# A GNN kernel's edge-count matrix: 32 source blocks of 100 instead of 40 of 80, laps of 8 groups, and two VectorE instructions a lap

## The chip, the cores and the metric

The kernel runs on one core of one Trainium2 chip. The metric is the device time of one execution in microseconds (us). "Before" was timed three times: 2426.53, 2431.27 and 2434.8 us, a median of 2431.27 us.

## The reference

There are 3125 nodes with 128 features and 103,125 edges, sorted by destination. Four graph layers run one after the other, each added to its input and layer-normalised:

```python
x = _layernorm(x + relu(segment_sum(edge_weight[:, None] * (x @ W0)[src], dst) + b0))        # GCN
x = _layernorm(x + gat(x))        # 4 heads, softmax over the edges into each dst, skip, layernorm
x = _layernorm(x + attention(x))  # Q,K,V, softmax over the edges into each dst; x + attn @ Wo
x = _layernorm(x + sage(x))       # two mean aggregations, relu between them, sigmoid at the end
```

All sums over edges are rewritten as products with dense 3200 x 3200 matrices (3125 padded to 3200, in 25 tiles of 128 rows). One holds how many edges lead from a source to a destination, one the sum of their weights.

## The kernel before

**Edge tables** (`edge_tables`, 0 to 81 us): the edge list is loaded, and for each group of WD = 3 destination rows the first 128 edges of the group are gathered. There are LAPS x LW = 1056 groups. A source number s is split into a high part hi = s // SL and a low part s % SL, with HI = 40 blocks of SL = 80. `k.near` holds five fields for each edge: the key (row in the group times HI plus hi, of KEYS = 120), the low part, and the edge weight as three bf16 pieces (PARTS = 3). The field is its outer dimension.

**Matrix build** (`build_matrices`, 81 to 450 us) runs LAPS = 88 laps of LW = 12 groups:

- DVE (`onehots`): one comparison makes the low one-hots (L483), one the key one-hots (L485), and three products (L489) multiply the low one-hots by the three weight pieces. Everything is double-buffered (RING = 2). The comparison waits on `used`, so for the PE of two laps before; the products wait on `lows`, which the first comparison sets.
- PE (`products`): for each group a matmul with the 128 key columns as weights and 160 moving columns (counts and first weight piece), and two more of 80 columns that add the other pieces. So 36 matmuls a lap, of which the last comes behind the check below.
- DVE and PE both call `beyond` in each lap: it reads two numbers of the table `k.before` into registers (L451) and compares them (L456). Only if some group has more than 128 edges does it do extra work, which doesn't occur in this execution. In the lap loop (`each_lap`, L446) two laps are unrolled.
- ACT (`copy_out`, L557) copies 120 partitions x 1920 results from PSUM to one of two `stage` buffers, after that buffer's last store has landed.
- SP (`store`, L566) stores the buffer in runs of 2 x 80 f32 (count and weight side by side, 640 bytes).

**Readers**: `aggregate` (449 to 610 us) multiplies the weight matrix with the features, 16 PE instructions for each of 25 tiles, from a ring of UN = 5 tiles. `gat_rows` and `attend_rows` load the counts, also in 25 tiles each. All three load through `load_rows` (L715), which gathers 80 f32 (320 bytes) at a time. The later `load_tiles` (L725) reads another matrix, which the change doesn't touch.

Of the kernel before, what the change touches and what calls it, by code (L numbers as in the profile page):

```python
# [14 lines left out]
BF16 = mybir.dt.bfloat16  # L15
I32 = mybir.dt.int32
I16 = mybir.dt.int16
ALU = mybir.AluOpType
# [3 lines left out]
P = 128  # L22
# [4 lines left out]
NP = NT * P  # L27
# [16 lines left out]
LASTN = E - FULL * P  # L44

WD = 3
HI = 40
SL = NP // HI
KEYS = WD * HI
LW = 12  # L50
LAPS = NP // (WD * LW)
ROWS = LAPS * LW * WD
WT = -(-(LAPS * LW + 1) // P)
NWP = WT * P
BATCHES = 3
PARTS = 3
RING = 2
# [49 lines left out]
def edge_tables(nc, k):  # L107

    with ExitStack() as ctx:
# [30 lines left out]
        start = sb("start", [P, WT])  # L140
# [3 lines left out]
        ids = sb("ids", [P, NWP], I32)  # L144
        weight = sb("weight", [P, NWP])
# [23 lines left out]
        WHOLE = (ECT - 1) * P  # L169
        TAIL = FULL - WHOLE  # L170
        N_PADS = 4
        N_CONSTS = 17
        BT = WT // BATCHES
        BW = BT * P

# [32 lines left out]
        def _(pool):  # L208
# [8 lines left out]
            pool.memset(k.ident[:, :], 0.0).then_inc(consts, 1)  # L217
            pool.memset(ahead[:, :], 0.0).then_inc(consts, 1)
            pool.memset(wrap[:, :], 0.0).then_inc(consts, 1)
            pool.memset(k.KEY[:, :, :, KEYS:P, :], 0.0).then_inc(consts, 1)  # L220
            pool.memset(k.zeros[:, :], 0.0).then_inc(consts, 1)
            pool.wait_ge(consts, 9)
            pool.affine_select(out=k.ident[:, :], in_=k.ident[:, :], compare_op=ALU.not_equal, fill=1.0,
                               base=0, pattern=[[-1, P]], channel_multiplier=1).then_inc(consts, 1)
            pool.affine_select(out=ahead[:, :], in_=ahead[:, :], compare_op=ALU.not_equal, fill=1.0,
# [4 lines left out]
                               base=P - 1, pattern=[[-1, P]], channel_multiplier=P).then_inc(consts, 1)  # L230
            pool.iota(base_i[:, :], pattern=[[KEYS, NWP]], base=0, channel_multiplier=0).then_inc(consts, 1)
            pool.iota(edge_i[:, :], pattern=[[P, ECOL]], base=0, channel_multiplier=1).then_inc(consts, 1)
            pool.iota(k.low_grid[:], pattern=[[1, SL], [0, 2]], base=0, channel_multiplier=0).then_inc(consts, 1)
            pool.iota(k.key_grid[:], pattern=[[1, KEYS], [0, 2]], base=0, channel_multiplier=0).then_inc(consts, 1)
            pool.wait_ge(rows_ready, 1)
            for t in range(WT):
                pool.indirect_dma_start(chunk_dst[:, t], None, k.dst.rearrange("(e a) -> e a", a=1),
# [7 lines left out]
                                        bass.IndirectOffsetOnAxis(ap=held_i[:, t:t + 1], axis=0)  # L245
                                        ).then_inc(k.own_in[t // BT], 16)
            pool.iota(k.iota_low[:, :], pattern=[[1, SL]], base=0, channel_multiplier=0)
            pool.iota(k.iota_key[:, :], pattern=[[1, P]], base=0, channel_multiplier=0)
            pool.memset(nought[:, :], 0.0).then_inc(noughts, 1)

        @block.vector
        def _(dve):
# [80 lines left out]
            for b in range(BATCHES):  # L333
                cols = slice(b * BW, (b + 1) * BW)
                dve.wait_ge(taken, 2 * (b + 1))
                unpack(ids[:, cols], weight[:, cols], BW, k.near[:, 0, cols], k.near[:, 1, cols],
                       [k.near[:, 2 + v, cols] for v in range(PARTS)], k.key_base[:, cols])

        @block.tensor
        def _(pe):  # L340
# [78 lines left out]
def build_matrices(nc, k):  # L419

    with ExitStack() as ctx:
        def sb(name, shape, dt=F32):
            return ctx.enter_context(nc.sbuf_tensor(name, shape, dt))

        def sem(name):
            return ctx.enter_context(nc.semaphore(name))

        OH = sb("bm_oh", [P, RING, LW // 2, 1 + PARTS, SL, 2], BF16)
        gate = sb("bm_gate", [P, 1])  # L430
        more_key = sb("bm_more_key", [P, P], BF16)
        more_oh = sb("bm_more_oh", [P, 1 + PARTS, SL], BF16)
        stage = sb("bm_stage", [KEYS, 2, LW, 2, SL])
        ps = ctx.enter_context(nc.psum_tensor("bm_ps", [P, 8, BANK], F32))
        used, lows, made, copied, more_step, more_made, more_used = map(
            sem, ("bm_used", "bm_lows", "bm_made", "bm_copied", "bm_more_step", "bm_more_made", "bm_more_used"))
        stored = [sem(f"bm_stored{s}") for s in range(2)]
        block = ctx.enter_context(nc.Block())
        WHY = "the tables' ranges lie inside the columns"
# [31 lines left out]
        @block.vector  # L471
        def _(dve):
            dve.sem_inc(more_used, 1)

            def onehots(lap, u, two):
                wide_low, wide_key = [P, LW // 2, SL, 2], [P, LW // 2, KEYS, 2]

                def spread(f, wide):
                    return (k.near[:, f, bass.ds(lap * LW, LW)].rearrange("p (a b) -> p a b", b=2).unsqueeze(2)
                            .to_broadcast(wide))  # L480

                dve.wait_ge(used, lap + 1)
                dve.tensor_tensor(OH[:, u, :, 0], k.low_grid[:].unsqueeze(1).to_broadcast(wide_low),  # L483
                                  spread(1, wide_low), ALU.is_equal).then_inc(lows, 1)
                dve.tensor_tensor(k.KEY[:, u, :, 0:KEYS], k.key_grid[:].unsqueeze(1).to_broadcast(wide_key),  # L485
                                  spread(0, wide_key), ALU.is_equal)
                dve.wait_ge(lows, lap + 1)
                for v in range(PARTS):
                    last = dve.tensor_tensor(OH[:, u, :, 1 + v], OH[:, u, :, 0], spread(2 + v, wide_low), ALU.mult)  # L489
                last.then_inc(made, 1)  # L490

                def more(at, w, c, b, i):
                    dve.wait_ge(more_used, at + 1)
                    dve.tensor_tensor(gate[:], k.edge_at[:, bass.ds(c, 1)], k.lim[:, bass.ds(w, 1)], ALU.is_ge
                                      ).then_inc(more_step, 1)
                    dve.tensor_scalar(more_key[:], k.iota_key[:], k.key_base[:, bass.ds(w, 1)],
                                      k.col_key[:, bass.ds(c, 1)], ALU.add, ALU.is_equal).then_inc(more_step, 1)
                    dve.tensor_scalar(more_oh[:, 0], k.iota_low[:], k.col_low[:, bass.ds(c, 1)], None, ALU.is_equal
                                      ).then_inc(more_step, 1)
                    dve.wait_ge(more_step, at * 3 + 3)  # L500
                    dve.tensor_scalar(more_key[:], more_key[:], gate[:], None, ALU.mult)
                    for v in range(PARTS):
                        last = dve.tensor_scalar(more_oh[:, 1 + v], more_oh[:, 0], k.col_parts[:, v, bass.ds(c, 1)], None,
                                                 ALU.mult)
                    last.then_inc(more_made, 1)

                beyond(dve, lap, more)

            each_lap(dve, onehots)

        @block.tensor
        def _(pe):
            pe.sem_inc(used, RING)
            pe.sem_inc(copied, 2)

            def products(lap, u, two):
                def place(i, v):
                    b, c = divmod(i, PER_BANK)
                    return ps[:, 4 * u + b, c * WIDE + SL * (v > 0):(c + 1) * WIDE]

                def body(i, planes):
                    a, b = divmod(i, 2)
                    for v in planes:
                        moving = OH[:, u, a, 0:2, :, b] if v == 0 else OH[:, u, a, 1 + v, :, b]
                        last = pe.matmul(place(i, v), k.KEY[:, u, a, :, b], moving, start=i % PER_BANK == 0 and v == 0,  # L525
                                         stop=True, skip_group_check=True)
                    return last

                pe.wait_ge(copied, lap + 1)
                pe.wait_ge(made, lap + 1)  # L530
                for i in range(LW - 1):
                    body(i, range(PARTS))
                body(LW - 1, range(PARTS - 1))

                def more(at, w, c, b, i):
                    pe.wait_ge(more_made, at + 1)
                    for v in range(PARTS):
                        out = ps[:, bass.ds(b + 4 * u, 1), bass.ds(i * WIDE + SL * (v > 0), WIDE - SL * (v > 0))]
                        out = out.rearrange("p b c -> p (b c)")
                        last = pe.matmul(out, more_key[:], more_oh[:, 0:2] if v == 0 else more_oh[:, 1 + v],  # L540
                                         start=False, stop=True, skip_group_check=True)
                    last.then_inc(more_used, 1)

                beyond(pe, lap, more)
                body(LW - 1, range(PARTS - 1, PARTS)).then_inc(used, 1)

            each_lap(pe, products)
# [1344 lines left out]
def program(nc, ins, out):  # L1892
# [16 lines left out]
    with ExitStack() as ctx:  # L1909
        def sb(name, shape, dt=F32):  # L1910
            return ctx.enter_context(nc.sbuf_tensor(name, shape, dt))
# [4 lines left out]
        with ExitStack() as edges:  # L1916
            def esb(name, shape, dt=F32):
                return edges.enter_context(nc.sbuf_tensor(name, shape, dt))

            k.chunk_in = [ctx.enter_context(nc.semaphore(f"chunk_in{b}")) for b in range(BATCHES)]  # L1920
            k.own_in = [ctx.enter_context(nc.semaphore(f"own_in{b}")) for b in range(BATCHES)]
            k.near = esb("near", [P, 2 + PARTS, NWP], BF16)
            k.before = esb("before_row", [1, NWP], I32)
            k.first = esb("first_row", [1, NWP], I32)
            k.lim = esb("limits", [P, NWP])
# [3 lines left out]
            k.col_parts = esb("col_parts", [P, PARTS, ECOL])  # L1929
            k.key_base = esb("key_base", [P, NWP])  # L1930
            k.iota_low = esb("iota_low", [P, SL], I16)
            k.iota_key = esb("iota_key", [P, P], I16)
            k.low_grid = esb("low_grid", [P, SL, 2], I16)
            k.key_grid = esb("key_grid", [P, KEYS, 2], I16)
            k.KEY = esb("key_onehots", [P, RING, LW // 2, P, 2], BF16)
            edge_tables(nc, k)
            build_matrices(nc, k)
        deg = sb("deg", [P, NT])
# [50 lines left out]
```

## Time and profile before

| | |
|---|---|
| timed runs | 2426.53, 2431.27, 2434.8 us |
| profiled execution's own time | 2439.62 us |
| its span (first to last instruction) | 2437.9 us |
| mean granted TensorE clock | 0.900 of full speed |
| busy share PE, PEld, DVE, ACT, POOL | 78%, 59%, 72%, 46%, 5% |
| first L483 to last build matmul | 81.3 to 440.9 us |
| first to last `aggregate` matmul start | 459.2 to 609.5 us |

The profile is one execution, so every duration in it comes from that one. Busy time is summed over the span; an idle stretch of an engine is put down to the engine or DMA whose semaphore event came last, which for a wait behind register work can name the wrong one. Matmuls overlap, so their durations don't add up to busy time.

### The profile page before, as it was taken

The numbers are of one execution on the slowest core, as the hardware profiler recorded it, in microseconds if no ns is written. First come the engines' busy times: TensorE is split into PE (matmuls) and PEld (weight loads), VectorE is DVE, ScalarE is ACT, GpSimd is POOL, SyncE is SP. The second block draws the span as 40 slices with busy tenths as digits, with TensorE's granted clock in tenths as the row PEclk, the third lists the DMA queues.
The fourth block names the chain that finished last, engine by engine and source line by source line (L and its number), as shares of the span: only waits on it lengthen the run. The fifth ranks groups of instructions, "written<-read, shape, count | busy, mean of one in ns | idle before, by whom it ended". The sixth has DMA issues, their size and how long they took to land. (4 is left out here: it accounts for less than half of the span.)

```text
span 2437.9 us, 44362 instructions
## 1 busy us (share of the span) xinstructions
PE 1902.0 (78%) x16121; PEld 1441.9 (59%) x16122; DVE 1753.2 (72%) x1874; ACT 1133.4 (46%) x1959; POOL 127.3 (5%) x225
## 2 busy tenths in 40 slices
PE   3456666699478888898888888873899999498794
PEld 2456555444456666676666667652688887354452
DVE  4887877100359999999999999855788885572375
ACT  1344444100257777677777777632666664101001
POOL 4000000000000000000000000000000000010120
PEclk6787877799689999999999999986899999699897
DMA  3488888999023443322444432211865650492492
GB/s 103 116 235 230 231 221 220 237 270 244 6 62 103 111 110 109 97 50 73 110 109 110 109 79 59 82 39 35 162 129 108 133 108 3 188 409 112 204 420 76
DMA packets 582353, 341.98 MB, mean 140 GB/s; under 512 B 397008, under 2 KB 574312, under 8 KB 575640
## 3 DMA queue, kind: packets, MB, share of 16 engines
q1 hardware_dynamic: 579928, 338.61, 50.4%
q0 software_dynamic: 720, 1.77, 0.3%
q10 hardware_dynamic: 1648, 0.83, 0.1%
q8 instruction: 37, 0.61, 0.1%
q14 instruction: 20, 0.16, 0.0%
HBM read 214.18 MB, written 127.01 MB: 140 GB/s over the span
## 5 line engine op out<-in xcount | busy, mean ns | idle before, releaser
L1207 ACT ACTIVATE exponentials<-gr_ps,att_cols 128x256 f32<-128x256 f32 (+1 forms) x1300 | 493.3, 491 | 185.1 <-PE gr_ps L1097 183.3
L1097 PE MATMUL gr_ps<-ident,gr_r 128*128 128x128 f32 x2500 | 381.8, 292 | 69.0 <-DVE gr_r L1315 67.0
L1097 PEld LDWEIGHTS gr_ps<-ident,gr_r 128*128 128x128 f32 x2500 | 284.1, 147 | 153.0 <-issue 130.8
L1128 PE MATMUL gr_ps<-exponentials,heads 128*33 128x128 f32 x5000 | 363.5, 277 | 14.1 <-DVE exponentials L1322 14.1
L1322 DVE SCALAR_TENSOR_TENSOR exponentials<-exponentials,gr_count_t 128x3072 f32<-128x3072 f32 (+1 forms) x104 | 349.0, 3355 | 21.9 <-ACT exponentials L1207 17.9
L1288 DVE CUSTOM_DVE_ANT_0 gr_unread<-gr_src_rows,gr_closed 128x3125 bf16<-128x3125 f32 (+1 forms) x100 | 344.2, 3442 | 17.0 <-ACT gr_closed L1200 16.6
L525 PE MATMUL bm_ps<-bm_oh,key_onehots 128*128 128x80 bf16 (+1 forms) x3168 | 228.9, 238 | 146.6 <-issue 119.4
L525 PEld LDWEIGHTS bm_ps<-bm_oh,key_onehots 128*128 128x128 bf16 x3168 | 202.7, 112 | 172.8 <-issue 169.3
L1128 PEld LDWEIGHTS gr_ps<-exponentials,heads 128*33 128x33 f32 x5000 | 254.1, 110 | 80.5 <-issue 55.9
L557 ACT ACTIVATE bm_stage<-bm_ps 120x1920 f32<-120x1920 f32 x88 | 156.0, 1773 | 220.8 <-DMA adjacency<-bm_stage 119.5
L798 PE MATMUL sage_ps<-sage_counts,sage_parts 128*128 128x400 bf16 x1200 | 207.4, 337 | 14.6 <-DVE sage_counts L832 14.6
L1315 DVE TENSOR_SCALAR gr_r<-gr_src_rows,gr_lift_u,gr_floor_u 128x3125 f32<-128x3125 f32 (+1 forms) x100 | 188.0, 1921 | 13.1 <-PE gr_ps L1097 7.5
L798 PEld LDWEIGHTS sage_ps<-sage_counts,sage_parts 128*128 128x128 bf16 x1200 | 118.6, 99 | 104.1 <-DVE sage_counts L832 16.0
L1546 PE MATMUL ar_ps<-KT,ar_left 128*128 128x400 f32 x400 | 147.1, 512 | 16.2 <-DVE ar_low_u L1637 14.7
L489 DVE TENSOR_TENSOR bm_oh<-bm_oh,near 128x960 bf16<-128x960 bf16 x264 | 157.4, 652 | 0.0
L698 PE MATMUL agg_gcn_ps<-agg_gcn_ring,agg_gcn_left 128*128 128x400 f32 x400 | 142.5, 512 | 14.3 <-DMA agg_gcn_ring<-adjacency 14.2
L1565 PEld LDWEIGHTS ar_ps<-ar_pt,X 128*128 128x128 f32 x1250 | 145.5, 192 | 11.5 <-ACT ar_pt L1609 4.5
L1565 PE MATMUL ar_ps<-ar_pt,X 128*128 128x128 f32 x1250 | 147.8, 275 | 0.0
L832 DVE CAST sage_counts<-sage_ring 128x3200 bf16<-128x3200 f32 x50 | 93.7, 1874 | 47.6 <-POOL sage_ring L788 47.6
L710 DVE COPY agg<-agg_gcn_ps 128x1600 f32<-128x1600 f32 x1 | 1.8, 1825 | 173.4 <-PE agg_gcn_ps L698 173.4
L698 PEld LDWEIGHTS agg_gcn_ps<-agg_gcn_ring,agg_gcn_left 128*128 128x128 f32 x400 | 75.6, 193 | 81.3 <-issue 30.6
L1609 ACT ACTIVATE ar_pt<-ar_ps 128x512 f32<-128x512 f32 (+1 forms) x175 | 84.0, 547 | 77.4 <-PE ar_ps L1555 77.4
(319 smaller groups left out, 1970.2 us busy)
## 6 DMA issues: line engine op xcount, KB each, us to landing
sage_ring<-count_by_source SPq DMA_DIRECT2D x50, 1600.0 KB, 9.3
adjacency<-bm_stage SPq DMA_DIRECT2D x88, 900.0 KB, 5.8
agg_gcn_ring<-adjacency SPq DMA_DIRECT2D x25, 1600.0 KB, 14.4
gr_count<-adjacency SPq DMA_DIRECT2D x25, 1600.0 KB, 9.3
ar_counts<-adjacency SPq DMA_DIRECT2D x25, 1600.0 KB, 9.1
count_by_source<-gr_count_t SPq DMA_DIRECT2D x12, 3200.0 KB, 16.7
fg_node<-gat_node_sums SPq DMA_DIRECT2D x1, 1650.0 KB, 6.3
count_by_source<-gr_count_t SPq DMA_DIRECT2D x1, 1600.0 KB, 7.1
```

What stands on the lines that cost most here:

```text
L489: last = dve.tensor_tensor(OH[:, u, :, 1 + v], OH[:, u, :, 0], spread(2 + v, wide_low), ALU.mult)
L525: last = pe.matmul(place(i, v), k.KEY[:, u, a, :, b], moving, start=i % PER_BANK == 0 and v == 0, stop=True, skip_group_check=True)
L557: act.activation(stage[:, u].rearrange("p (b w) v c -> p b (w v c)", b=BANKS), ps[0:KEYS, BANKS * u:BANKS * (u + 1), 0:PER_BANK * WIDE], A ...
L698: last = pe.matmul(ps[:, b, 0:CW], left[:, u, :], ring[:, u, b * CW:(b + 1) * CW], start=False, stop=True, skip_group_check=True)
L798: last = pe.matmul(ps[:, b, 0:CW], parts[:, u, i, :], counts[:, u, b * CW:(b + 1) * CW], start=False, stop=True, skip_group_check=True)
L1097: last = pe.transpose(ps[:, i % RINGS, c:c + P], r[:, j, s * P:(s + 1) * P], k.ident[:])
L1128: last = pe.matmul(ps[j * PAIR:j * PAIR + C + 1, 7, 0:P], heads[:, h, s, :], e[:, s, j * P:(j + 1) * P], start=s == 0, stop=s == NT - 1, s ...
L1207: last = act.activation(e[:, s, 0:w], ps[:, i % RINGS, c:c + w], ACT.Exp, bias=cols[:, h, s:s + 1])
L1288: dve.tensor_tensor_reduce(out=unread[:, 0:n], in0=src_rows[:, h, 0:n], in1=closed[:, j, 0:n], scale=1.0, scalar=FLOOR, op0=ALU.subtract, ...
L1315: last = dve.tensor_scalar(r[:, j, 0:n], src_rows[:, h, 0:n], lift_u[:, h, j:j + 1], floor_u[:, h, j:j + 1], ALU.add, ALU.max)
L1322: dve.scalar_tensor_tensor(part, part, 1.0, count_t[:, first:last, 0:w], ALU.min, ALU.mult).then_inc(weighed, 1)
L1565: last = pe.matmul(ps[:, 7, 0:P], k.X[:, first + j, :], pt[:, i, j * P:(j + 1) * P], start=first + j == 0, stop=first + j == NT - 1, skip_ ...
```

## The change

- HI goes from 40 to 32 and so SL from 80 to 100 and KEYS from 120 to 96. The stored run is 2 x 100 f32 (800 bytes), the run read by `load_rows` 100 f32 (400 bytes).
- LW goes from 12 to 8, LAPS from 88 to 132. The number of groups stays 1056 and `ROWS` 3168.
- The key one-hots get the same width (100) as the low ones and lie in the same tile, `hot`, and both come from one comparison against one grid. The three products become one instruction. That one waits for the comparison in front of it.
- The matmul's weights are 100 columns instead of 128, its moving columns 200, 100 and 100 instead of 160, 80 and 80; results lie in 100 PSUM partitions, of which 96 are copied.
- `k.near` gets the layout [group of 8 edges' columns, field, column], so that one access pattern spans several fields; the edge tables write it in pieces of 8.
- Two iotas and a memset go from the POOL queue.

```diff
-HI = 40
+HI = 32
-LW = 12
-LAPS = NP // (WD * LW)
+LW = 8
+LAPS = 2 * (NP // (2 * WD * LW))
...
-            pool.memset(k.KEY[:, :, :, KEYS:P, :], 0.0).then_inc(consts, 1)
...
-            pool.iota(k.low_grid[:], pattern=[[1, SL], [0, 2]], base=0, channel_multiplier=0).then_inc(consts, 1)
-            pool.iota(k.key_grid[:], pattern=[[1, KEYS], [0, 2]], base=0, channel_multiplier=0).then_inc(consts, 1)
+            pool.iota(k.grid[:], pattern=[[1, SL], [0, 2]], base=0, channel_multiplier=0).then_inc(consts, 1)
...
-            pool.iota(k.iota_key[:, :], pattern=[[1, P]], base=0, channel_multiplier=0)
...
-                unpack(ids[:, cols], weight[:, cols], BW, k.near[:, 0, cols], k.near[:, 1, cols],
-                       [k.near[:, 2 + v, cols] for v in range(PARTS)], k.key_base[:, cols])
+                mine = [k.near[:, b * (BW // LW):(b + 1) * (BW // LW), f, :] for f in range(2 + PARTS)]
+                unpack(ids[:, cols], weight[:, cols], BW, mine[0], mine[1], mine[2:], k.key_base[:, cols])
...
-        OH = sb("bm_oh", [P, RING, LW // 2, 1 + PARTS, SL, 2], BF16)
+        hot = sb("bm_hot", [P, RING, 2 + PARTS, LW // 2, SL, 2], BF16)
...
+                def over(fields):
+                    return [P, (fields.stop - fields.start) * (LW // 2), SL, 2]
+
+                def spread(fields):
+                    mine = k.near[:, bass.ds(lap, 1), fields].rearrange("p l f (a b) -> p (l f a) b", b=2)
+                    return mine.unsqueeze(2).to_broadcast(over(fields))
+
+                def planes(fields):
+                    return hot[:, u, fields].rearrange("p f a c b -> p (f a) c b")
+
+                both, parts = slice(0, 2), slice(2, 2 + PARTS)
                 dve.wait_ge(used, lap + 1)
-                dve.tensor_tensor(OH[:, u, :, 0], k.low_grid[:].unsqueeze(1).to_broadcast(wide_low),
-                                  spread(1, wide_low), ALU.is_equal).then_inc(lows, 1)
-                dve.tensor_tensor(k.KEY[:, u, :, 0:KEYS], k.key_grid[:].unsqueeze(1).to_broadcast(wide_key),
-                                  spread(0, wide_key), ALU.is_equal)
-                dve.wait_ge(lows, lap + 1)
-                for v in range(PARTS):
-                    last = dve.tensor_tensor(OH[:, u, :, 1 + v], OH[:, u, :, 0], spread(2 + v, wide_low), ALU.mult)
-                last.then_inc(made, 1)
+                dve.tensor_tensor(planes(both), k.grid[:].unsqueeze(1).to_broadcast(over(both)), spread(both), ALU.is_equal
+                                  ).then_inc(compared, 1)
+                dve.wait_ge(compared, lap + 1)
+                low = hot[:, u, 1].rearrange("p a c b -> p (a c b)").unsqueeze(1)
+                dve.tensor_tensor(planes(parts), low.to_broadcast([P, PARTS, LW * SL]), spread(parts), ALU.mult
+                                  ).then_inc(made, 1)
...
+                        moving = hot[:, u, 1:3, a, :, b] if v == 0 else hot[:, u, 2 + v, a, :, b]
+                        last = pe.matmul(ps[0:SL, BANKS * u + bank, c * WIDE + SL * (v > 0):(c + 1) * WIDE],
+                                         hot[:, u, 0, a, :, b], moving, start=c == 0 and v == 0, stop=True,
+                                         skip_group_check=True)
...
-            k.near = esb("near", [P, 2 + PARTS, NWP], BF16)
+            k.near = esb("near", [P, NWP // LW, 2 + PARTS, LW], BF16)
```

## Rows read from the trace of the kernel before

**Rows 1.** Groups of instructions, 81 to 450 us; line, operation, count, busy, mean ns, idle before.

```profile
L525 PE MATMUL bm_ps<-bm_oh,key_onehots 128*128 128x80 bf16 (+1 forms) x3168 | 228.9, 238 | 146.6 <-issue 119.4 <-DVE bm_oh L489 26.5
L489 DVE TENSOR_TENSOR bm_oh<-bm_oh,near 128x960 bf16<-128x960 bf16 x264 | 157.4, 652 | 0.0
L557 ACT ACTIVATE bm_stage<-bm_ps 120x1920 f32<-120x1920 f32 x88 | 156.0, 1773 | 220.8 <-DMA adjacency<-bm_stage 119.5 <-PE bm_ps L525 101.3
L485 DVE TENSOR_TENSOR key_onehots<-key_grid,near 128x1440 bf16<-128x1440 int16 x88 | 79.3, 902 | 0.0
L483 DVE TENSOR_TENSOR bm_oh<-low_grid,near 128x960 bf16<-128x960 int16 x88 | 57.9, 658 | 76.6 <-PE bm_ps L525 74.0 <-issue 1.4 <-PEq L513 1.0
```

**Rows 2.** Windows: build stage; stretch, length, busy by engine, PE clock, DMA share, GB/s.

```profile
81.20:441.20 360.00, 228.88 (x3168) 202.73 (x3168) 279.76 (x440) 154.26 (x88) 0.00 (x0) 0.80 0.81 220
```

**Rows 3.** Timeline, 199 to 217 us; start, duration, instruction, idle before.

```profile
199.53 0.66 DVE L483 TENSOR_TENSOR bm_oh<-low_grid,near 128x960 bf16<-128x960 int16 x1 [1.33 <-PE bm_ps L525]
202.64 0.65 DVE L483 TENSOR_TENSOR bm_oh<-low_grid,near 128x960 bf16<-128x960 int16 x1
202.86 1.88 PE L525 MATMUL bm_ps<-bm_oh,key_onehots 128*128 128x160 bf16 x35 [0.50 <-DVE bm_oh L489]
207.33 0.66 DVE L483 TENSOR_TENSOR bm_oh<-low_grid,near 128x960 bf16<-128x960 int16 x1 [1.52 <-PE bm_ps L525]
...
208.73 1.79 DVE L489 TENSOR_TENSOR bm_oh<-bm_oh,near 128x960 bf16<-128x960 bf16 x3
...
211.04 0.66 DVE L483 TENSOR_TENSOR bm_oh<-low_grid,near 128x960 bf16<-128x960 int16 x1 [0.52 <-PE bm_ps L525]
...
214.80 0.66 DVE L483 TENSOR_TENSOR bm_oh<-low_grid,near 128x960 bf16<-128x960 int16 x1 [0.58 <-PE bm_ps L525]
```

**Rows 4.** DVE's queue in the lap 207.2 to 210.9 us; ns min/median/max, first and last start.

```profile
L451 DVEq TENSOR_LOAD <-before_row x2: 431/706/980, 208.5 to 209.9; - x2
L456 DVEq COMPARE_BRANCH  x1: 56/56/56, 210.6 to 210.6; - x1
L483 DVEq FUSED_REGOPS  x1: 75/75/75, 210.9 to 210.9; - x1
```

**Rows 5.** DVE's queue in the next lap, 210.9 to 214.6 us.

```profile
L489 DVEq FUSED_REGOPS  x3: 57/57/57, 211.7 to 212.0; - x3
L451 DVEq TENSOR_LOAD <-before_row x2: 303/462/620, 212.3 to 213.4; - x2
L446 DVEq COMPARE_BRANCH  x1: 66/66/66, 214.3 to 214.3; - x1
```

**Rows 6.** Line 451 over the whole span, the queues of DVE and PE.

```profile
L451 DVEq TENSOR_LOAD <-before_row x176: 302/556/1370, 82.5 to 435.8; - x176
L451 PEldq TENSOR_LOAD <-before_row x176: 298/624/1487, 86.2 to 440.0; - x176
```

**Rows 7.** Line 451, 81 to 91 us, before and at the first store.

```profile
L451 DVEq TENSOR_LOAD <-before_row x6: 304/312/556, 82.5 to 90.5; - x6
```

**Rows 8.** The first comparison and the staging tile, whole span.

```profile
L483 DVE TENSOR_TENSOR bm_oh<-low_grid,near x88: 650/659/660, 81.3 to 433.5; 128x960 bf16<-128x960 int16 x88
L566 SPq DMA_DIRECT2D adjacency<-bm_stage x88: 329/330/377, 90.5 to 443.1; - x88
...
  DMA adjacency<-bm_stage: 119.5, 54
...
DMA to landing us min/median/max: 5.4/5.8/7.0
```

**Rows 9.** Groups of instructions, whole span: an ACT copy of 1536, two weight loads.

```profile
L1220 ACT ACTIVATE gr_count_t<-gr_ps 128x1536 f32<-128x1536 f32 x50 | 70.1, 1449 | 40.9 <-PE gr_ps L1106 40.9
L525 PEld LDWEIGHTS bm_ps<-bm_oh,key_onehots 128*128 128x128 bf16 x3168 | 202.7, 112 | 172.8 <-issue 169.3
L698 PEld LDWEIGHTS agg_gcn_ps<-agg_gcn_ring,agg_gcn_left 128*128 128x128 f32 x400 | 75.6, 193 | 81.3 <-issue 30.6
```

**Rows 10.** Windows of `aggregate`: three tiles from a full ring, fifteen in steady state.

```profile
467.30:483.40 16.10, 16.10 (x49) 9.04 (x48) 0.00 (x0) 0.00 (x0) 0.88 (x3) 1.00 1.25 272
508.40:598.55 90.15, 84.53 (x240) 44.42 (x240) 0.00 (x0) 0.00 (x0) 3.62 (x13) 1.00 1.24 272
```

**Rows 11.** ACT waits for the first count tiles of `attend_rows`, timeline.

```profile
1706.19 2.96 ACT L1598 ACTIVATE ar_closed<-ar_counts,ar_big 128x3200 bf16<-128x3200 f32 x1 [15.27 <-DMA ar_counts<-adjacency]
```

**Rows 12.** DVE waits for DMA in the edge tables, groups of instructions, 0 to 200 us.

```profile
L288 DVE CAST dst_f<-dst_i 128x903 f32<-128x903 int32 x1 | 0.6, 630 | 3.2 <-DMA dst_i<-in_dst_dram 3.2
L283 DVE TENSOR_TENSOR near<-scratch,near 128x384 bf16<-128x384 f32 x3 | 1.7, 559 | 0.1
```

More of the change, by code:

```diff
@@ L171, in edge_tables @@
         N_PADS = 4
-        N_CONSTS = 17
+        N_CONSTS = 15
         BT = WT // BATCHES
@@ L219, in _ @@
             pool.memset(wrap[:, :], 0.0).then_inc(consts, 1)
-            pool.memset(k.KEY[:, :, :, KEYS:P, :], 0.0).then_inc(consts, 1)
             pool.memset(k.zeros[:, :], 0.0).then_inc(consts, 1)
-            pool.wait_ge(consts, 9)
+            pool.wait_ge(consts, 8)
             pool.affine_select(out=k.ident[:, :], in_=k.ident[:, :], compare_op=ALU.not_equal, fill=1.0,
@@ L427, in sem @@
             return ctx.enter_context(nc.semaphore(name))
-        OH = sb("bm_oh", [P, RING, LW // 2, 1 + PARTS, SL, 2], BF16)
+        hot = sb("bm_hot", [P, RING, 2 + PARTS, LW // 2, SL, 2], BF16)
         gate = sb("bm_gate", [P, 1])
-        more_key = sb("bm_more_key", [P, P], BF16)
+        more_key = sb("bm_more_key", [P, SL], BF16)
         more_oh = sb("bm_more_oh", [P, 1 + PARTS, SL], BF16)
@@ L434, in build_matrices @@
         ps = ctx.enter_context(nc.psum_tensor("bm_ps", [P, 8, BANK], F32))
-        used, lows, made, copied, more_step, more_made, more_used = map(
-            sem, ("bm_used", "bm_lows", "bm_made", "bm_copied", "bm_more_step", "bm_more_made", "bm_more_used"))
+        used, compared, made, copied, more_step, more_made, more_used = map(
+            sem, ("bm_used", "bm_compared", "bm_made", "bm_copied", "bm_more_step", "bm_more_made", "bm_more_used"))
         stored = [sem(f"bm_stored{s}") for s in range(2)]
@@ L475, in onehots @@
             def onehots(lap, u, two):
[L476 to L480, printed above, removed]
-                dve.wait_ge(used, lap + 1)
-                dve.tensor_tensor(OH[:, u, :, 0], k.low_grid[:].unsqueeze(1).to_broadcast(wide_low),
-                                  spread(1, wide_low), ALU.is_equal).then_inc(lows, 1)
-                dve.tensor_tensor(k.KEY[:, u, :, 0:KEYS], k.key_grid[:].unsqueeze(1).to_broadcast(wide_key),
-                                  spread(0, wide_key), ALU.is_equal)
-                dve.wait_ge(lows, lap + 1)
-                for v in range(PARTS):
-                    last = dve.tensor_tensor(OH[:, u, :, 1 + v], OH[:, u, :, 0], spread(2 + v, wide_low), ALU.mult)
-                last.then_inc(made, 1)
+                def over(fields):
[6 more added lines that the diff above has]
+                both, parts = slice(0, 2), slice(2, 2 + PARTS)
+                dve.wait_ge(used, lap + 1)
+                dve.tensor_tensor(planes(both), k.grid[:].unsqueeze(1).to_broadcast(over(both)), spread(both), ALU.is_equal
[4 more added lines that the diff above has]
+                                  ).then_inc(made, 1)
                 def more(at, w, c, b, i):
@@ L495, in more @@
                                       ).then_inc(more_step, 1)
-                    dve.tensor_scalar(more_key[:], k.iota_key[:], k.key_base[:, bass.ds(w, 1)],
+                    dve.tensor_scalar(more_key[:], k.iota_low[:], k.key_base[:, bass.ds(w, 1)],
                                       k.col_key[:, bass.ds(c, 1)], ALU.add, ALU.is_equal).then_inc(more_step, 1)
@@ L516, in products @@
             def products(lap, u, two):
-                def place(i, v):
-                    b, c = divmod(i, PER_BANK)
-                    return ps[:, 4 * u + b, c * WIDE + SL * (v > 0):(c + 1) * WIDE]
                 def body(i, planes):
                     a, b = divmod(i, 2)
+                    bank, c = divmod(i, PER_BANK)
                     for v in planes:
-                        moving = OH[:, u, a, 0:2, :, b] if v == 0 else OH[:, u, a, 1 + v, :, b]
-                        last = pe.matmul(place(i, v), k.KEY[:, u, a, :, b], moving, start=i % PER_BANK == 0 and v == 0,
-                                         stop=True, skip_group_check=True)
+                        moving = hot[:, u, 1:3, a, :, b] if v == 0 else hot[:, u, 2 + v, a, :, b]
+                        last = pe.matmul(ps[0:SL, BANKS * u + bank, c * WIDE + SL * (v > 0):(c + 1) * WIDE],
+                                         hot[:, u, 0, a, :, b], moving, start=c == 0 and v == 0, stop=True,
+                                         skip_group_check=True)
                     return last
@@ L537, in more @@
                     for v in range(PARTS):
[L538 to L541, printed above, removed]
+                        out = ps[0:SL, bass.ds(b + BANKS * u, 1), bass.ds(i * WIDE + SL * (v > 0), WIDE - SL * (v > 0))]
+                        last = pe.matmul(out.rearrange("p b c -> p (b c)"), more_key[:],
+                                         more_oh[:, 0:2] if v == 0 else more_oh[:, 1 + v], start=False, stop=True,
+                                         skip_group_check=True)
                     last.then_inc(more_used, 1)
@@ L1931, in program @@
             k.iota_low = esb("iota_low", [P, SL], I16)
[L1932 to L1935, printed above, removed]
+            k.grid = esb("grid", [P, SL, 2], I16)
             edge_tables(nc, k)
```

## The prediction

> **What bounds the kernel now.** The change touches the build of the matrix, and through the layout the stages that read it, so I read the groups of the build first. 88 laps run from the first L483 at 81.3 to the last at 433.5 us [rows 8]: 352.2 / 87 = 4.05 us a lap, 356 us in all, 15% of the span. Neither the groups nor the window name an engine that is full: DVE is busy for 280 of 360 us, PE 229, ACT 154, the DMA engines 81% [rows 1, 2]. ACT waits 119.5 us for stores and 101.3 us for PE; DVE waits 74 us "for PE" [rows 1].
>
> The last is misleading. Follow one lap [rows 3, 4]. The comparisons start at 207.33 and the three products are through at 208.73 + 1.79 = 210.52, yet the next comparison starts at 211.04. PE isn't what holds it: DVE's own queue read a table entry from 209.9 for 0.43 us, branched at 210.6 and came to the next L483 at 210.9. The queue takes its items in turn: it dispatches the five instructions, the products only once the first comparison is complete, then makes `beyond`'s two reads and the branch, and only then enters the next lap. That lap took 3.71 us, of which the reads were 0.431 + 0.980 = 1.41 and the rest 2.30. The next lap, with the loop's branch, took 3.76 us: reads 0.92, rest 2.84 [rows 3, 5]. So a lap costs DVE's queue (2.30 + 2.84) / 2 = 2.57 us plus two reads. A read took 0.30 us before the first store [rows 7] and 0.556 us at the median of the stage, up to 1.37 [rows 6]. Were there no other wait, 4.05 - 2.57 = 1.48 us would be two reads; twice the median is 1.11. DVE's queue is thus busy for 3.7 to 4.05 of 4.05 us. PE's queue has the same reads (median 0.624, rows 6) and its own 36 matmuls; it isn't far behind. A staging buffer's round is copy 1.77, issue about 0.2, landing 5.8 us: 7.8 for two laps, 3.9 a lap [rows 1, 8]. Three loops of nearly one length, then, of which the first has a cost per lap, whatever a lap holds.
>
> **The change part by part.** I work against the profiled execution, 2439.6 us.
>
> *DVE in a lap.* By L483 and L485 an element costs (902 - 658) / 480 = 0.508 ns [rows 1]. The one comparison of 2 x 8 x 100 = 1600 elements takes 658 + 640 x 0.508 = 983 ns, the one product of 2400 takes 652 + 1440 x 0.508 = 1384 ns. That is 2.37 us of engine time a lap where the five took 0.66 + 0.90 + 3 x 0.65 = 3.52: fewer instructions, but the elements per group rise from 440 to 500. In the queue the product waits for a comparison of 0.98 instead of 0.66 us (+0.325), and two dispatches go; three of them start from 211.7 to 212.0, so 0.13 each [rows 5] (-0.26). The rest of a lap goes from 2.57 to 2.635 us. The two reads and the branch stay, because they are per lap. The product (1.38 us) lies beside them and costs nothing; it would cost only if the reads and the branch, 1.1 us plus at least 0.6, were gone.
>
> *The reads.* The floor is 2 x 0.30 = 0.61 us [rows 7], the ceiling the 1.48 of above. They are longer while stores run, and a store now has 48 packets an engine instead of 90 or more in a lap that is little shorter, so I take the middle, 1.05. Lap: 2.635 + 1.05 = 3.69 us; 132 laps 486 us, against 356: **+130 us**. Ends: 132 x 3.24 = 428 (+72) and 132 x 4.11 = 543 (+187).
>
> *PE in a lap.* 35 matmuls ran in 1.88 us for 12 groups of 320 columns [rows 3]; 8 groups of 400 columns are 3200 instead of 3840, so about 1.6 us warm and twice that at the lower clock level. Its period was within 4.05 with 12 matmuls more. It fits beside 3.69, and it gets slack, since the matmuls of a lap can start after 2.4 us of DVE's lap and not after 3.3. Zero; bounds 0 to +0.23 us a lap, inside the ends above. Should weights of 100 columns load more slowly, see below.
>
> *ACT and the store.* A copy of 1536 took 1449 ns, of 1920 1773 [rows 1, 9]: 0.84 ns an element, so 1600 take 1.50 us. The DMA share of 0.81 over 360 us and 16 engines for 88 x 120 x 12 = 126,720 runs [rows 2] is 36.8 ns a run of 640 bytes; 90 runs an engine are 3.3 us, and 5.8 - 3.3 = 2.5 us of the landing are fixed. A run of 800 bytes costs between 36.8 (by the run) and 46 ns (by the byte); 48 of them 1.8 to 2.2 us. Landing 4.5 us, round 1.5 + 0.2 + 4.5 = 6.2, so 3.1 us a lap: hidden under 3.69. Without that cover the stage would take 132 x 3.1 = 409 us.
>
> *Tail of the stage.* The last copy is 0.3 us shorter, the last landing 1.3: -1.6, say -2.
>
> *Readers.* Three tiles from a full ring took 16.1 us, 5.37 each; in steady state 15 tiles took 90.15, 6.01 each [rows 10], with PE idle in between at full clock: there the loads set the pace. A tile is 5120 runs of 320 bytes and becomes 4096 of 400. By the run that is 4.8 us, so PE's 5.37 would bound; by the byte nothing changes. About 20 tiles are paced so: 0 to -13 us; I take -10, nearer to the run, as the engines move 272 GB/s here in runs half the size of the store's. In `gat_rows` and `attend_rows` only the first loads are exposed, the clearest by 15.3 us [rows 11]; a tenth of it is -2 (0 to -4) in both together.
>
> *Edge tables.* The iotas and the memset that go leave DVE waiting for `dst_i` 3.2 us longer than for POOL [rows 12], so 0. The writes of `near` in pieces of 8 are made from f32 input at 559 ns for 384 elements, 1.45 ns each: slow already, so 0; were each of the 15 twice as long, +8.
>
> Sum: +130 - 2 - 10 - 2 = +116 us, 2555.6 us for a twin of the profiled execution. That one lay 8.3 us above the median, so I forecast 2431.3 + 116 = **2547 us**.
>
> **The rivals.**
>
> *A, the cost goes by the group (chance 0.07), and the change wins.* If DVE's and PE's queue work is hidden and what paces a lap is what it stores and computes, a lap of 8 groups takes 8/12 of 4.05 = 2.70 us and the stage stays at 356. The readers' and the tail's 14 us are left: 2417 us. For it: ACT waited for stores in 54 of 88 laps [rows 8]. Against it: laps of 3.71 and 3.76 us that the queue explains to the end. It decides from a lap below (356 + 14) / 132 = 2.80 us; the queue's fixed part alone is 2.6, and with two of the quickest reads 3.24.
>
> *B, quiet reads (0.15).* If the loops lock so that the reads fall between the stores, the lap is 3.24: +72 - 14, 2489 us. The lap from 199.53 to 202.64 took 3.11 us in the midst of the stage [rows 3], so quick laps exist. Against it: the median read of the stage is nearly twice the quiet one.
>
> *C, the staging round bounds (0.05).* If the reads take less than I think and the round of 3.1 us is the longest loop: 409 - 356 - 14 = +39, 2470 us.
>
> *D, weight loads (0.05).* A bf16 load of 128 columns averages 112 ns, an f32 load of the same 193 [rows 9]. If 100 columns lose the quick form, and a load's extra 50 to 90 ns can't hide behind matmuls of 100 columns, 24 of them add 1.2 to 2.2 us to PE's lap of at most 4.05 - 12 x 0.054 = 3.4, and a lap of about 5 us gives 660 - 356 - 14 = +290, 2721 us. The Trainium skill, "TensorE: Matmul & The Clock Gate", section "Weight-path perf modes", states just that condition: the quick weight load is on only for 128 weights that aren't f32. What no row says is whether the slow one shows; loads already lie beside matmuls (35 in a stretch of 1.88 us is 54 ns each, half of a load's own 112), hence the small chance.
>
> **How the numbers follow.** Main case 0.68. The range 2475 to 2625 takes in B and all but the last part of the main case's ends (2489 to 2604, and 20 us above for waits of DVE on the stores) and leaves out A, C and D, 0.17, and a little of the tails. A difference of 0.3% (7 us) is what a measurement can tell from none. Faster by more: 0.07 (A). Within: 0.02 (between A and C). Slower: 0.91.
>
> **What would show it.** In the profile after: 132 L451 pairs, still two reads a lap, of 0.3 to 1 us; from one comparison to the next 3.5 to 3.9 us with a DVE that is busy for only 2.3 of them and idle "for PE"; the two DVE instructions at 0.98 and 1.38 us; the ACT copy at 1.50, landings of 4 to 4.5 us with ACT waiting mostly for PE; tiles of `aggregate` at 5.4 to 5.6 us. The prediction is wrong if the comparison-to-comparison time is below 3 us, or if PE's stretch of 23 matmuls takes over 3 us at full clock.

## The result and the profile after

The changed kernel takes 2592.7 us at the median (2591.3 to 2593.8, four runs), the kernel before 2432.7 in the same comparison: a ratio of 1.066 [1.064, 1.068], 160 us slower. The forecast was 2547 (2475 to 2625), slower with a chance of 0.91. The profiled execution has a span of 2590.3 us, 152.4 more than the one before.

Groups of the build stage in the profile after, which answer to [rows 1] and the bf16 weight load of [rows 9]; line, operation, count, then busy us, mean ns, then idle us before it:

```profile
L522 PE MATMUL bm_ps<-bm_hot 128*100 128x100 bf16 (+1 forms) x3168 | 311.7, 264 | 220.8 <-DVE bm_hot L489 127.2
L522 PEld LDWEIGHTS bm_ps<-bm_hot 128*100 128x100 bf16 x3168 | 276.5, 158 | 256.1 <-issue 211.3
L555 ACT ACTIVATE bm_stage<-bm_ps 96x1600 f32<-96x1600 f32 x132 | 197.9, 1500 | 335.5 <-PE bm_ps L522 335.5
L485 DVE TENSOR_TENSOR bm_hot<-grid,near 128x1600 bf16<-128x1600 int16 x132 | 131.0, 992 | 178.7 <-issue 170.6
L489 DVE TENSOR_TENSOR bm_hot<-bm_hot,near 128x2400 bf16<-128x2400 bf16 x132 | 185.8, 1408 | 18.8
```

DVE's two instructions are busy for 317 us and idle between them for 197, of which 171 are now "issue": the engine waited for nothing that the profile shows. ACT no longer waits for a store at all; PE, when it waits, waits mostly for DVE (127 of 221 us). The windows of the build stage and of fifteen tiles of `aggregate` (as [rows 2, 10]; length, busy by engine, clock, DMA share, GB/s) and the comparison and the store over the whole span (as [rows 8]; ns min/median/max, first and last start):

```profile
81.20:597.00 515.80, 311.44 (x3167) 276.33 (x3167) 316.51 (x264) 196.45 (x131) 0.00 (x0) 0.76 0.57 156
661.00:751.20 90.20, 84.54 (x240) 44.36 (x240) 0.00 (x0) 0.00 (x0) 3.72 (x13) 1.00 1.30 272
```

```profile
L485 DVE TENSOR_TENSOR bm_hot<-grid,near x132: 991/993/994, 80.9 to 591.7; 128x1600 bf16<-128x1600 int16 x132
...
L564 SPq DMA_DIRECT2D adjacency<-bm_stage x132: 317/317/366, 88.4 to 599.4; - x132
...
DMA to landing us min/median/max: 4.0/4.0/4.6
```

A lap is (591.7 - 80.9) / 131 = 3.90 us with 8 groups, where it was 4.05 with 12. The difference of the spans splits so: from the first to the last comparison +158.6 us less 0.4 for an earlier start; from there to the first `aggregate` matmul -4.4; `aggregate` -0.8; all behind it -0.6.

Two laps, read as [rows 4, 5] were. The comparisons start at 200.91, 204.60 and 208.68. First the reads of DVE's queue in the lap from 200.8 to 204.5 with the loop's branch, then those from 204.5 to 208.6 us:

```profile
200.91 0.99 DVE L485 TENSOR_TENSOR bm_hot<-grid,near 128x1600 bf16<-128x1600 int16 x1 [1.55 <-issue]
...
204.60 0.99 DVE L485 TENSOR_TENSOR bm_hot<-grid,near 128x1600 bf16<-128x1600 int16 x1 [1.15 <-issue]
...
208.68 0.99 DVE L485 TENSOR_TENSOR bm_hot<-grid,near 128x1600 bf16<-128x1600 int16 x1 [1.54 <-issue]
```

```profile
L448 DVEq TENSOR_LOAD <-before_row x2: 303/438/573, 202.2 to 203.1; - x2
...
L443 DVEq COMPARE_BRANCH  x1: 66/66/66, 204.1 to 204.1; - x1
```

```profile
L448 DVEq TENSOR_LOAD <-before_row x2: 318/860/1401, 205.8 to 207.7; - x2
L453 DVEq COMPARE_BRANCH  x1: 56/56/56, 208.3 to 208.3; - x1
```

3.69 - (0.303 + 0.573) = 2.81 us and 4.08 - (0.318 + 1.401) = 2.36 us. With the reads taken off, nearly every lap of the stage is one of these two numbers (10th to 90th percentile 2.36 to 2.36 and 2.82 to 2.82). So DVE's queue waits for no other engine, and what varies is the reads, 1.31 us a lap on average. In the kernel before it did wait: the same subtraction gives 2.29 to 4.4 us there, 2.80 on average, with reads of 1.25 us a lap.

### The profile page after: what moved, and what is told of

Same layout as the page of the kernel before. It is cut to its first block and busy times, and to the rows that moved or that the text cites. A ratio compares the mean times of both kernels' runs of the same rounds, so it can differ in the third digit from the quotient of the medians.

```text
span 2590.3 us, 45415 instructions
## 1 busy us (share of the span) xinstructions
PE 1984.6 (77%) x16121; PEld 1516.1 (59%) x16122; DVE 1790.3 (69%) x1698; ACT 1175.5 (45%) x2003; POOL 126.1 (5%) x222
## 5 line engine op out<-in xcount | busy, mean ns | idle before, releaser
L522 PE MATMUL bm_ps<-bm_hot 128*100 128x100 bf16 (+1 forms) x3168 | 311.7, 264 | 220.8 <-DVE bm_hot L489 127.2
L522 PEld LDWEIGHTS bm_ps<-bm_hot 128*100 128x100 bf16 x3168 | 276.5, 158 | 256.1 <-issue 211.3
L555 ACT ACTIVATE bm_stage<-bm_ps 96x1600 f32<-96x1600 f32 x132 | 197.9, 1500 | 335.5 <-PE bm_ps L522 335.5
L485 DVE TENSOR_TENSOR bm_hot<-grid,near 128x1600 bf16<-128x1600 int16 x132 | 131.0, 992 | 178.7 <-issue 170.6
L489 DVE TENSOR_TENSOR bm_hot<-bm_hot,near 128x2400 bf16<-128x2400 bf16 x132 | 185.8, 1408 | 18.8
```

The lines of the kernel that those rows point to most:

```text
L489: dve.tensor_tensor(planes(parts), low.to_broadcast([P, PARTS, LW * SL]), spread(parts), ALU.mult).then_inc(made, 1)
L522: last = pe.matmul(ps[0:SL, BANKS * u + bank, c * WIDE + SL * (v > 0):(c + 1) * WIDE], hot[:, u, 0, a, :, b], moving, start=c == 0 and v = ...
L555: act.activation(stage[:, u].rearrange("p (b w) v c -> p b (w v c)", b=BANKS), ps[0:KEYS, BANKS * u:BANKS * (u + 1), 0:PER_BANK * WIDE], A ...
```

## The experiments

Lap means the time from one first comparison to the next, over the whole stage. Unless a ratio is given, a kernel ran once, beside a run of the kernel before on the same chip at 2433.7 to 2436.9 us.

### The check taken off one queue or both

```diff
-                beyond(dve, lap, more)
```

and the same for `pe`.

> The changed kernel without the check on VectorE: DVE no longer reads the table twice a lap and no longer branches (leaves out the handling of groups with over 128 edges, of which this input has none; PE keeps its check). Theory Q (DVE's queue, with two reads and a branch per lap, sets the lap of 3.90 us): DVE's lap falls to its engine time of about 2.5 us, the next longest loop takes over, the staging round (1.5 + 0.2 + 4.0) / 2 = 2.85 or PE's queue at about 3.0; lap 3.0 to 3.1, so 105 to 120 us less, about 2475 to 2490 us. Rival P (PE sets the lap, by its own check or by weights of 100 columns that load slowly): lap stays at 3.9, 2585 to 2595 us. Rival S (the stores set the lap): the same, 2585 to 2595.

> The changed kernel without the check on TensorE's queue, DVE keeps its own (leaves out the matmuls of groups with over 128 edges, of which there are none). Theory Q: DVE's queue is untouched, lap 3.9, within 8 us of the changed kernel's 2593. Rival P: the lap falls by up to 0.9 us, 2480 to 2540. Rival S: no change.

> The changed kernel with the check on neither DVE nor PE. Theory Q: PE's lap is then about 1.7 us warm and under 3 cold, DVE 2.5, so the staging round of 2.85 us is the longest: lap 2.85 to 3.0, 2460 to 2475 us. Rival P (slow weight loads hold PE up): a lap well above 3.0 with PE's stretch of matmuls filling it, 2500 or more. Rival S: 2593.

> The kernel before with the check on neither DVE nor PE. Theory Q with three loops of nearly one length: the staging round of 3.9 us is left, lap 4.05 to 3.85-3.95, so 9 to 18 us less, 2415 to 2425. Rival (DVE's queue alone set it, the store round has slack): lap down to DVE's engine time of 3.3, 66 us less, 2365. Rival (nothing in the queues mattered): 2432.

| kernel | us | lap |
|---|---|---|
| changed, no check on DVE | 2496.5 | 3.16 |
| changed, no check on PE | 2558.0 | 3.66 |
| changed, on neither | 2464.2 | 2.89 |
| before, on neither | 2425.2 | 3.85 |

Without DVE's check 96 us go, and the lap falls from 3.90 to 3.16 us. ACT's idle time then still stands under PE (234 of 239 us), whose queue keeps its own check. Without any check the idle time of ACT moves to the stores, in both kernels: the staging round is what is left. These are the ACT idle rows of the changed kernel and of the kernel before without checks (us, times):

```profile
  DMA adjacency<-bm_stage: 183.9, 130
  PE bm_ps L521: 20.5, 1
```

```profile
  DMA adjacency<-bm_stage: 179.5, 83
  PE bm_ps L524: 27.6, 4
```

Two expectations failed. Without DVE's check the time was to be 2475 to 2490 us and is 6 us more. And taking the check from PE alone was to change nothing and took 35 us. DVE's fixed part (the lap less its reads) stayed at 2.36 and 2.82 us; its reads went from 1.31 to 1.07 us a lap. So the check on PE does not make DVE wait, but it changes how long DVE's reads take. The likely way is that PE's lap decides when a store is issued; the table under "Small stores" bears on it.

### Laps of 8 groups in the old layout

```diff
-LW = 12
-LAPS = NP // (WD * LW)
+LW = 8
+LAPS = 2 * (NP // (2 * WD * LW))
```

> The kernel before with LW = 8, so 132 laps of 8 groups instead of 88 of 12, and nothing else changed: 40 blocks of 80, five VectorE instructions, weights of 128 columns. Theory Q (the cost is per lap): fixed part of a lap 2.57 less 0.16 for the shorter first comparison = 2.41, reads 1.0 to 1.3, lap 3.4 to 3.7, stage 450 to 490 us instead of 356: about 2550 us (2530 to 2570). Rival L (what cost the time is the new layout, with its wider one-hots, slow weight loads or 800-byte runs): 2432 within 15 us.

2585.5 us, lap 3.84, with 128-column weights, five DVE instructions and 640-byte runs. The lap count alone makes 149 of the 160 us. The fixed part is 2.40 us (expected 2.41), the reads 1.44 (expected 1.0 to 1.3), so it came 15 us above the range. TensorE's granted clock stood at its lower level (0.50, 1.2 GHz) through the whole stage of this run, where it was 0.76 in the changed kernel, and DVE's queue still waited for nobody: its laps less the reads are 2.13 and 2.67 us. The window, 90 to 580 us:

```profile
90.00:580.00 490.00, 315.20 (x3068) 268.83 (x3067) 288.18 (x636) 157.32 (x128) 0.00 (x0) 0.50 0.61 160
```

### The comparison split in two

```diff
-                dve.tensor_tensor(planes(both), k.grid[:].unsqueeze(1).to_broadcast(over(both)), spread(both), ALU.is_equal
-                                  ).then_inc(compared, 1)
+                for fields in (slice(1, 2), slice(0, 1)):
+                    step = dve.tensor_tensor(planes(fields), k.grid[:].unsqueeze(1).to_broadcast(over(fields)),
+                                             spread(fields), ALU.is_equal)
+                    if fields.start:
+                        step.then_inc(compared, 1)
```

> The changed kernel with its one comparison split in two, low one-hots first, and only that one waited for by the product; three VectorE instructions a lap. Theory Q: the queue's wait falls from 0.99 to 0.59 us, one dispatch of 0.13 comes back: fixed part 2.59 -> 2.32, lap 3.9 -> 3.6 if the reads stay at 1.3; 36 us less, about 2557 us (2525 to 2590, since the reads move against the stores). Rival E (what counts is the number of instructions or the engine time of VectorE): 5 to 20 us more, 2598 to 2612.

2562.4 us, lap 3.69. More instructions and more engine time, yet 30 us less: the fixed part fell from 2.59 to 2.19, the reads rose from 1.31 to 1.50. The fall is 0.40 us, nearly the whole difference between waiting for a comparison of 0.99 us and for one of 0.58; the 0.13 us that I had added for one more dispatch did not show. Merging the two comparisons had put the whole 0.99 us ahead of the reads in the queue.

### Small stores

```diff
-                sp.dma_start(k.adj_w[:, bass.ds(lap * LW, LW), :], stage[:, u].rearrange("p w v c -> p w (v c)")
+                sp.dma_start(k.adj_w[0:16, bass.ds(lap * LW, LW), :], stage[0:16, u].rearrange("p w v c -> p w (v c)")
```

> The changed kernel that stores only 16 of the 96 partitions in each lap (leaves out five sixths of the matrix; the matrix is cleared ahead of the stage by 100 stores of zeros, some 250 to 330 us that come on top and are not part of the comparison; to be compared is the lap). Theory R (a table read is long because a store runs): reads near 0.30 to 0.4 us, the fixed part still 2.59, lap 3.2 to 3.4. Rival (the reads of the two engines hinder each other, or an engine's own work does): reads stay at 0.65 on average, lap 3.9.

Lap 3.42, a little over the range. The fixed part is 2.59 as ever, the reads 0.83 us a lap. The rows of DVE's reads, of this kernel and of the changed one:

```profile
L449 DVEq TENSOR_LOAD <-before_row x264: 301/324/910, 249.1 to 698.2; - x132
```

```profile
L448 DVEq TENSOR_LOAD <-before_row x264: 301/420/1460, 82.1 to 594.2; - x132
```

Sorting DVE's reads by how long after the latest issue of a store they began gives the pattern, here for the changed kernel, for the same kernel without the check on PE, and for the one before; mean us, with their number:

```
begun after issue:       0-0.4      0.4-0.8    0.8-1.2    1.2-1.6    1.6-2.0    2.0-2.4    2.4-2.8    2.8-3.2    3.2-3.6
changed kernel           0.32 (17)  0.41 (14)  1.34 (40)  1.09 (13)  1.04 (32)  0.72 (28)  0.44 (24)  0.31 (25)  0.30 (67)
changed, no check on PE  0.31 (31)  0.37 (11)  1.17 (12)  1.09 (16)  1.04 (21)  0.69 (36)  0.46 (42)  0.31 (12)  0.30 (75)
before                   0.31 (22)  0.60 (44)  0.84 (9)   -          1.37 (1)   1.09 (3)   0.98 (16)  0.93 (18)  0.44 (21)
```

In the changed kernel a read that begins 0.8 to 2 us after a store's issue takes 1.0 to 1.3 us at the mean and ends 2.4 to 2.8 us after the issue; from 2.8 us on a read takes 0.30 us. In the kernel before, with nearly twice the runs a store, the slow stretch lasts longer: 28 reads begun 3.6 to 4.4 us after the issue still average 0.65 us. The rival that the reads of DVE and PE hinder each other doesn't fit: without PE's reads those of DVE cost nearly the same at the same distance from a store, only fewer of them begin 0.8 to 2.4 us after it (33% for 43%). Since all loops repeat once a lap, a read can meet the slow stretch in lap after lap. By which path the store holds a read up is not shown.

### The loads of the first aggregation

```diff
-                    load_rows(sp, ring[:, u, :], matrix, t).then_inc(loaded[u], 16)
+                    sp.dma_start(ring[:, u, :].unsqueeze(1), k.adj_flat[:, bass.ds(t, 1)]).then_inc(loaded[u], 16)
```

> The changed kernel whose first aggregation loads whole rows of 12,800 bytes instead of runs of 400 (it reads the same number of bytes but other places of the matrix, so that layer is computed from other numbers). Theory B (the loads go by bytes, not by runs): a tile still takes 6.0 us, total within 5 us of 2593. Rival (by runs): a tile at PE's own 5.4 us, about 13 us less, 2580.

> The changed kernel whose first aggregation loads runs of 512 bytes with gaps of 512, 3200 runs a tile instead of 4096 of 400 (same bytes, other places, so that layer is computed from other numbers). Runs of 320 and of 400 bytes both gave 6.02 us a tile, whole rows 5.37. Theory T (there is a threshold between 400 and 512 bytes; the Trainium skill, DMA: Bandwidth & Descriptors, Specifications, names 512 bytes as the least transfer at full rate): a tile at PE's 5.37 us, 13 us less, about 2580 us. Rival G (every gathered load goes at 272 GB/s, whatever the run): 6.0 us a tile, 2593.

Whole rows: 2573.3 us, 5.37 us a tile, PE never idle. Runs of 512 bytes (the same edit with 25 runs a row): 2583.7 us, 5.65 us a tile. Windows of the two kernels, the first of whole rows while the ring of tiles still fills, to be set beside the 272 GB/s of [rows 10] (320 bytes) and of the window above (400 bytes):

```profile
620.00:640.00 20.00, 20.00 (x61) 11.38 (x60) 0.00 (x0) 0.00 (x0) 1.17 (x4) 1.00 0.95 383
640.00:700.00 60.00, 60.00 (x180) 33.90 (x180) 0.00 (x0) 0.00 (x0) 3.22 (x11) 1.00 0.85 306
```

```profile
660.00:740.00 80.00, 79.86 (x230) 42.20 (x228) 0.00 (x0) 0.00 (x0) 3.52 (x12) 1.00 1.21 290
```

The rows' 306 GB/s is only what PE consumes; before that they went at 383. Whole rows came out as the rival by runs had it, but neither theory holds: gathered loads aren't bound by bytes alone, since whole rows are faster, nor by the run, since 320 and 400 bytes go at the same 272 GB/s. The run of 512 bytes came between its two expectations as well: 290 GB/s, short of the 305 that 5.37 us a tile would need. The rule of the Trainium skill ("DMA: Bandwidth & Descriptors", Specifications) of 512 bytes for the full rate agrees in direction; at 512 the full rate isn't reached here.

What sets the 272 GB/s is open. SP's queue is a candidate that no experiment took apart from the DMA engines: the issue of a gathered load stands in it for 5.7 us at the median (5.4 with 512 bytes), nearly the whole tile, and that of whole rows for 0.33. Against it, the first gathered issue took only 0.66 us:

```profile
L713 SPq DMA_DIRECT2D agg_gcn_ring<-adjacency x25: 660/5745/5979, 604.2 to 742.2; - x25
L681 SPq DMA_DIRECT2D agg_gcn_ring<-adjacency x25: 332/333/393, 601.1 to 718.1; - x25
```

### One check ahead of the laps, and four staging buffers

```diff
+        def by_need(eng, step):
+            total = eng.value_load(k.before[0:1, LAPS * LW:LAPS * LW + 1], min_val=0, max_val=LAPS * LW * NCH)
+            with eng.If(total < 1):
+                each_lap(eng, lambda lap, u, two: step(lap, u, False))
+            with eng.If(total > 0):
+                each_lap(eng, lambda lap, u, two: step(lap, u, True))
...
-        stage = sb("bm_stage", [KEYS, 2, LW, 2, SL])
+        stage = sb("bm_stage", [KEYS, STAGES, LW, 2, SL])
```

> The kernel before with one check ahead of the laps: DVE and PE each read the total number of edges beyond 128 once; if it is zero they run laps without reads or branch, else the laps as they were. Full function. Theory Q: as with the check left out on both, the staging round of 3.9 us bounds: 2425 us (2418 to 2430), 0.3 to 0.6% faster than before. Rival (the second copy of the loops costs code loading that shows): 2430 to 2440.

> The same with four staging buffers instead of two. Theory Q with the three loops: the check is gone and the staging round is halved, so what is left is DVE's engine time, 0.58 + 0.82 + 1.79 and about 0.1 = 3.3 us a lap, and the DMA engines' own 90 runs x 36.8 ns = 3.3: lap 3.35 to 3.5, 35 to 48 us less than with two buffers: 2378 to 2392 us. Rival (the stores go no faster than one per 3.9 us, since the DMA engines are full): 2425.

> The changed kernel with the one check ahead and four staging buffers. Full function. Theory Q: a lap at DVE's engine time, 0.99 + 0.14 + 1.41 and about 0.1 = 2.65 us, against 2.90 with the check left out and two buffers: 132 x 0.25 = 33 us less than 2464, about 2431 us (2420 to 2445), slower than the kernel before with the same two edits by 40 to 55 us. Rival (with the per-lap work gone the wider layout is worth as much or more): 2375 to 2400.

| kernel | us | ratio to before | lap |
|---|---|---|---|
| before, one check | 2425.2 | 0.996 [0.994, 0.998] | 3.86 |
| before, one check, four buffers | 2363.1 | 0.971 [0.969, 0.972] | 3.12 |
| changed, one check, four buffers | 2402.3 | 0.986 [0.985, 0.988] | 2.46 |

Both loops had to go. The check alone leaves the staging round; with four buffers as well the kernel before gets to 2363.1 us, the best of all versions, with the full function. A lap of 3.12 is DVE's own work, 100% busy, with TensorE's clock at the upper level, 2.4 GHz, throughout. The stores are close behind: the DMA share is 1.00 where it was 0.81, a store lands 10.3 us after its issue instead of 5.8, and ACT still waits 72 us for stores. Windows, 100 to 350 us of that kernel and 100 to 400 us of the changed one with the same edits:

```profile
100.00:350.00 250.00, 153.85 (x2889) 144.82 (x2886) 249.75 (x403) 140.71 (x80) 0.00 (x0) 1.00 1.00 291
```

```profile
100.00:400.00 300.00, 200.40 (x2933) 188.67 (x2934) 282.54 (x246) 183.70 (x123) 0.00 (x0) 1.00 0.91 250
```

Both fell below their expectation, by 15 and 18 us: my laps were about 0.2 us too long, of which 0.1 was for dispatch. In fact the next comparison even starts a little before the last product is through (201.73 + 1.78 = 203.51), as in this lap of the kernel before with the two edits:

```profile
201.73 1.78 DVE L498 TENSOR_TENSOR bm_oh<-bm_oh,near 128x960 bf16<-128x960 bf16 x3
203.44 0.64 DVE L492 TENSOR_TENSOR bm_oh<-low_grid,near 128x960 bf16<-128x960 int16 x1
```

The changed layout is 39 us slower even so. Its DVE has 500 elements a group against 440, and a bubble of 0.14 us a lap between comparison and product, 19 us in 132 laps.

## Why the prediction was right, and where its sizes were off

- **What bounds.** Right: DVE's queue, through the two reads and the branch of each lap, set the lap. Three loops of nearly one length before, of which one has a cost per lap: the checks taken off left both kernels at the staging round, 3.85 and 2.89 us (said: 3.9 and 3.1; the new store landed in 4.0 us and not in 4.5).
- **Fixed part of a lap.** Said 2.635 us, measured 2.59 (2.36 and 2.82); the instructions 0.983 and 1.384, measured 0.993 and 1.408. The 0.04 come from the laps with the loop's branch, which take 0.45 us more than the others, where it was 0.54 in the two laps that I had read.
- **The reads.** The term that was mis-sized: said 1.05 us, halfway between floor and ceiling, because smaller stores would hinder less; measured 1.31. In the kernel before they were 1.25 us a lap, so that they were to fall by 0.2 and rose by 0.06; the ceiling of 1.48 held 0.23 us of other waits. A store of 768 runs instead of 1440 has a shorter slow stretch, but a read costs by its place after the store, and the first of DVE's two fell into the stretch more often (0.91 us at the mean, the second 0.40; before 0.74 and 0.50). 132 x 0.26 is +34 us, the fixed part -6: stage +158.6 for +130. That the time lies in the range is owed to its width, which took in the whole way from floor to ceiling. The argument for the middle, the size of the store, holds by itself (small stores: 0.83), but it left out where in the lap a read begins.
- **Readers.** Said -10 us, measured -0.8. A longer run of 400 bytes brought nothing; for "nearer to the run" there was no row with another run of the same load, and the experiments show that the pace isn't linear in the runs. The first wait of `attend_rows` went from 15.27 to 14.45 us, about half of the tenth that I had said, and all stages behind `aggregate` together gave -0.6 for the -2.
- **Tail and edge tables.** The tail was -4.4 for -2, and the edge tables' 0 was -0.4. The sum of the profiled executions is +152.4 for +116.
- **Rival A**, cost by the group, fell: DVE's queue did not hide. **B** (quiet reads) needed 0.61 us; even small stores left 0.83. **C**, the staging round, appeared only when the checks were gone, at 2464 us for 2470. **D**: the weight load of 100 bf16 columns did lose speed, 158 against 112 ns at the mean and 122 against 95 at the least, and it didn't show: with 128-column weights and 8 groups the lap was 3.84, and the changed kernel's 23 matmuls take 1.59 us at full clock, as was said:

```profile
301.54 1.59 PE L522 MATMUL bm_ps<-bm_hot 128*100 128x200 bf16 x23 [1.15 <-DVE bm_hot L489]
```

- The idle time of DVE was to be put down to PE; it stands under "issue".

## What to carry to other kernels

Before making laps smaller, read the engine's queue in one lap, not only its busy time: subtract the loads of registers and look whether the rest is a constant. Going from 88 to 132 laps in the old layout cost 149 us of the 160, because each lap brings its queue work (2.40 us) and two reads (1.44) along. In the kernel before, hoisting a data-dependent check out of the loop was worth 0.4% until the next loop of equal length, the double buffer, was widened too; then it was 2.9%. Merging instructions doesn't shorten a queue in which the next one waits for the merged result.

## What was unexpected of the hardware

- A load of one number from on-chip memory into a queue's register takes 0.30 us, and 1.0 to 1.3 us at the mean, up to 1.46, when it begins 0.8 to 2 us after SP has issued a store (changed kernel).
- Gathered loads of 320- and 400-byte runs ran at the same 272 GB/s, 512-byte runs at 290, and whole rows at 306, no more than PE took, and at 383 while the ring filled.
- An f32 store of 96 x 8 runs of 800 bytes lands in 4.0 us, one of 120 x 12 runs of 640 in 5.8.
